# A new table of jobs in the slots of an attention loop, K one batch later, and three pairs of squares on GpSimd

## What is computed

```
x = x + 0.5 * (real(ifft(fft(LN(x)) @ W)) + bias)     # called F1 here
x = x + attention(LN(x))                              # 16 heads of 8, on the left 128 features
x = x + 0.5 * (real(ifft(fft(LN(x)) @ W)) + bias)     # called F2 here
```

## Time and profile before

| | |
|---|---|
| median of three runs | 313.4 us |
| profiled execution | 312.38 us |
| its span | 310.5 us |
| TensorE matmuls busy | 294.8 us (95%) |
| ScalarE busy | 257.6 us (83%) |
| VectorE busy | 190.5 us (61%) |
| GpSimd busy | 98.3 us (32%) |
| granted TensorE clock | full throughout |
| chain that ended last: TensorE / DMA / VectorE / ScalarE | 75% / 9% / 5% / 5% |

### The profile page before, as it was taken

The page is one execution under the profiler, slowest core; times in us unless marked ns, Lnnn a source line. Parts: engine busy times, 40 slices in busy tenths (PEclk is TensorE's granted clock), DMA queues, the critical chain, the costliest instruction groups (busy, mean ns, idle before and its releaser), DMA issues.

```text
span 310.5 us, 8810 instructions
## 1 busy us (share of the span) xinstructions
PE 294.8 (95%) x3440; PEld 112.5 (36%) x3443; DVE 190.5 (61%) x552; ACT 257.6 (83%) x285; POOL 98.3 (32%) x113
## 2 busy tenths in 40 slices
PE   8887999899998999999999999999999999998996
PEld 5633333233332333333333333334333333322333
DVE  1688546747775678657776678567755643370255
ACT  2117998898997889998998989998999999999921
POOL 6562531223604053223604251313600340034005
PEclk9999999999999999999999999999999999999999
DMA  7935615573462762665453663554372464112102
GB/s 192 337 137 192 218 65 153 195 270 133 139 217 83 245 208 103 208 204 217 155 192 129 231 205 112 198 172 143 131 238 104 138 205 170 38 68 70 37 34 70
DMA packets 25891, 49.33 MB, mean 159 GB/s; under 512 B 2032, under 2 KB 14192, under 8 KB 24048
## 3 DMA queue, kind: packets, MB, share of 16 engines
q1 hardware_dynamic: 25152, 48.26, 46.0%
q10 hardware_dynamic: 688, 0.40, 0.8%
HBM read 31.08 MB, written 17.56 MB: 157 GB/s over the span
## 4 chain that ended last, share of the span: by engine, by line
PE 75%; DMA 9%; DVE 5%; ACT 5%; issue 3%; POOL 3%; SPq 0%; ACTq 0%; POOLq 0%
PE ot L828 28%; PE misc L719 26%; PE scores L799 15%; ACT probs L669 5%; DMA leftT<-left_scr 4%; DMA q_scr<-qp 2%; PE scores L719 2%; DMA QS<-q_scr 2%; DMA left_scr<-left_blocks 1%; POOL x L553 1%; PE scores L686 1%; PE scores L693 1%; DVE left_blocks L966 1%; DVE lh L957 1%; POOL rstd L550 1%
## 5 line engine op out<-in xcount | busy, mean ns | idle before, releaser
L669 ACT ACTIVATE probs<-scores 128x1024 f32<-128x1024 f32 x256 | 243.8, 1028 | 20.6 <-PE scores L799 20.3
L828 PE MATMUL ot<-probs,VS 128*32 128x512 f32 x1024 | 133.9, 594 | 2.9 <-ACT probs L669 2.3
L799 PE MATMUL scores<-QS,KS 32*128 32x512 f32 x512 | 64.7, 495 | 3.0 <-DMA QS<-q_scr 1.3
L799 PEld LDWEIGHTS scores<-QS,KS 32*128 32x128 f32 x512 | 24.5, 181 | 109.8 <-ACT probs L669 101.0
L828 PEld LDWEIGHTS ot<-probs,VS 128*32 128x32 f32 x1024 | 30.6, 109 | 25.8 <-ACT probs L669 5.0
L563 POOL TENSOR_TENSOR x_out<-x,half_bias 128x512 f32<-128x512 f32 x7 | 9.0, 1292 | 88.8 <-DVE x L1012 88.8
L548 POOL TENSOR_SCALAR veps<-mv 128x4 f32<-128x4 f32 (+1 forms) x25 | 6.1, 242 | 95.9 <-DVE mv L946 95.9
L1017 DVE SCALAR_TENSOR_TENSOR x_out<-misc,rstd,x_out 128x256 f32<-128x256 f32 x28 | 13.5, 484 | 33.7 <-PE misc L719 30.2
L719 PE MATMUL misc<-half_ffn,xT 128*32 128x256 f32 x448 | 32.1, 386 | 0.0
L719 PE MATMUL misc<-half_ffn,xT_in 128*32 128x256 f32 x400 | 27.1, 385 | 1.4 <-DVE half_ffn L1193 1.3
L550 POOL TENSOR_TENSOR rstd<-veps,power 128x4 f32<-128x4 f32 (+1 forms) x25 | 25.3, 1013 | 2.1
(11 more groups left out here) (125 smaller groups left out, 260.0 us busy)
## 6 DMA issues: line engine op xcount, KB each, us to landing
KS<-k_scr SPq DMA_DIRECT2D x14, 512.0 KB, 4.9
QS<-q_scr SPq DMA_DIRECT2D x14, 512.0 KB, 4.6
x_in<-x SPq DMA_DIRECT2D x8, 512.0 KB, 5.1
xT_in<-x_t SPq DMA_DIRECT2D x8, 512.0 KB, 6.4
k_scr<-kp SPq DMA_DIRECT2D x8, 512.0 KB, 3.0
q_scr<-qp SPq DMA_DIRECT2D x8, 512.0 KB, 4.4
x_scr<-x_blocks SPq DMA_DIRECT2D x7, 512.0 KB, 2.9
xT<-x_scr SPq DMA_DIRECT2D x7, 512.0 KB, 4.7
```

The source lines that it names most:

```text
L669: nc.scalar.activation(probs[u % PRING][:, :, :], scores[u % SRING][:, :, :], ACT.Exp, scale=SCORE_SCALE).then_inc(exp_done, 1)
L799: last = mm(scores[(u + j // 2) % SRING][:, j % 2, :], KS[b % 2][rows, slot, kt * P:(kt + 1) * P].bitcast(F32R), QS[b % 2][rows, slot, :]. ...
L828: last = mm(ot[COL * j:COL * (j + 1), :], VS[b % 2][:, kt, h, :], probs[(u + j // 2) % PRING][:, j % 2, :], start=s % 8 == 0, stop=s % 8 == 7)
```

## The change

The tables are new. Offset 1 is the next batch and 2 the one after it. K of the next batch is made in slots 4 and 6 (STEADY) or 4 and 5 (LATE), where it was made for the batch after the next in slots 14 and 15. F1 and F2 tiles are spread as halves over other slots. SP's loop issues x2 and xT first, then k_out, k_in, q_out and q_in together, and the left half last. The guard's branch moves from slot 12 to 13 in batches 1 to 5, and from 13 to 12 in batch 0. `left_half` goes to slots 12 and 13, the statistics of the next x to slots 6 and 8. The squares of k and q of batches 1, 2 and 7 go from ScalarE to GpSimd; those of batches 3 to 6 stay on ScalarE in slots 8 and 11.

```diff
--- before.py
+++ after.py
@@ -66,28 +66,31 @@
 
 
 
-STEADY = {0: [("F2_3a", -2, LEFT), ("F2_3", -2, LEFT)], 1: [("F1_0a", 2, LEFT), ("F1_0", 2, LEFT)],
+STEADY = {0: [("F2_3", -2, LEFT), ("F1_0a", 2, RIGHT)], 1: [("F1_0", 2, RIGHT)],
           2: [("WO_0", -1, LEFT), ("WO_1", -1, RIGHT)], 3: [("WO_2", -1, LEFT), ("WO_3", -1, RIGHT)],
-          4: [("F1_1a", 2, LEFT), ("F1_1", 2, LEFT)], 5: [("F1_2a", 2, LEFT), ("F1_2", 2, LEFT)],
-          6: [("F1_3a", 2, LEFT), ("F1_3", 2, LEFT)], 7: [("QT_0", 1, LEFT)], 8: [("QT_1", 1, LEFT)],
-          9: [("V_0", 1, RIGHT), ("V_1", 1, LEFT)], 10: [("N", 1, RIGHT), ("F2_0a", -1, LEFT)], 11: [("F2_0", -1, LEFT)],
-          12: [("F2_1a", -1, LEFT), ("F2_1", -1, LEFT)], 13: [("F2_2a", -1, LEFT), ("F2_2", -1, LEFT)],
-          14: [("KT_0", 2, RIGHT)], 15: [("KT_1", 2, RIGHT)]}
-
-FIRST = {**STEADY, 0: [("F1_0a", 2, LEFT), ("F1_0", 2, LEFT)], 1: []}
+          4: [("KT_0", 1, RIGHT), ("F1_1a", 2, LEFT)], 5: [("F1_1", 2, LEFT), ("V_0", 1, RIGHT)],
+          6: [("KT_1", 1, RIGHT), ("F1_2a", 2, LEFT)], 7: [("F1_2", 2, LEFT), ("V_1", 1, RIGHT)], 8: [("QT_0", 1, RIGHT)],
+          9: [("QT_1", 1, RIGHT), ("F1_3a", 2, LEFT)], 10: [("F1_3", 2, LEFT)],
+          11: [("N", 1, RIGHT), ("F2_0a", -1, LEFT)], 12: [("F2_0", -1, LEFT), ("F2_1a", -1, RIGHT)], 13: [("F2_1", -1, RIGHT)],
+          14: [("F2_2a", -1, LEFT), ("F2_2", -1, LEFT)], 15: [("F2_3a", -1, LEFT)]}
+
+FIRST = {**STEADY, 0: [("F1_0a", 2, LEFT), ("F1_0", 2, LEFT)], 1: [("F1_1a", 2, LEFT), ("F1_1", 2, LEFT)],
+         4: [("F1_2a", 2, LEFT)], 5: [("F1_2", 2, LEFT), ("V_0", 1, RIGHT)], 6: [("QT_0", 1, RIGHT)], 7: [("QT_1", 1, RIGHT)],
+         8: [("F1_3a", 2, LEFT)], 9: [("F1_3", 2, LEFT)], 10: [("V_1", 1, RIGHT)]}
 
 BEGIN = {3: [("LT", 1, LEFT)], 4: [("KT_0", 1, RIGHT), ("F1_0a", 2, LEFT)], 5: [("F1_0", 2, LEFT), ("QT_0", 1, RIGHT)],
          6: [("KT_1", 1, RIGHT), ("F1_1a", 2, LEFT)], 7: [("F1_1", 2, LEFT), ("QT_1", 1, RIGHT)],
-         8: [("F1_2a", 2, LEFT), ("F1_2", 2, LEFT)], 9: [("F1_3a", 2, LEFT), ("F1_3", 2, LEFT)],
-         10: [("V_0", 1, RIGHT), ("V_1", 1, LEFT)], 11: [("N", 1, RIGHT)], 12: [("LT", 2, LEFT)],
-         13: [("KT_0", 2, RIGHT)], 14: [("KT_1", 2, LEFT)]}
-
-LATE = {0: [("F2_3a", -2, LEFT), ("F2_3", -2, LEFT)],
+         8: [("F1_2a", 2, LEFT), ("F1_2", 2, LEFT)], 9: [("V_0", 1, RIGHT), ("F1_3a", 2, LEFT)],
+         10: [("F1_3", 2, LEFT), ("N", 1, RIGHT)], 11: [("V_1", 1, RIGHT)],
+         13: [("LT", 2, LEFT)], 14: [("KT_0", 2, RIGHT)], 15: [("KT_1", 2, RIGHT)]}
+
+LATE = {0: [("F2_3", -2, LEFT)],
         2: [("WO_0", -1, LEFT), ("WO_1", -1, RIGHT)], 3: [("WO_2", -1, LEFT), ("WO_3", -1, RIGHT)],
-        5: [("QT_0", 1, LEFT)], 6: [("QT_1", 1, LEFT)], 7: [("V_0", 1, RIGHT)], 8: [("V_1", 1, LEFT)],
-        9: [("F2_0a", -1, LEFT)], 10: [("F2_0", -1, LEFT), ("N", 1, RIGHT)], 11: [("F2_1a", -1, LEFT)], 12: [("F2_1", -1, LEFT)],
-        13: [("F2_2a", -1, LEFT)], 14: [("F2_2", -1, LEFT)]}
-END = {0: [("F2_3a", -2, LEFT), ("F2_3", -2, LEFT)],
+        4: [("KT_0", 1, RIGHT)], 5: [("KT_1", 1, RIGHT)], 6: [("QT_0", 1, RIGHT)], 7: [("QT_1", 1, RIGHT)],
+        8: [("V_0", 1, RIGHT)], 9: [("V_1", 1, RIGHT), ("F2_0a", -1, LEFT)], 10: [("F2_0", -1, LEFT), ("N", 1, RIGHT)],
+        11: [("F2_1a", -1, LEFT)], 12: [("F2_1", -1, LEFT)],
+        13: [("F2_2a", -1, LEFT)], 14: [("F2_2", -1, LEFT)], 15: [("F2_3a", -1, LEFT)]}
+END = {0: [("F2_3", -2, LEFT)],
        2: [("WO_0", -1, LEFT), ("WO_1", -1, RIGHT)], 3: [("WO_2", -1, LEFT), ("WO_3", -1, RIGHT)],
        9: [("F2_0a", -1, LEFT)], 10: [("F2_0", -1, LEFT)], 11: [("F2_1a", -1, LEFT)], 12: [("F2_1", -1, LEFT)],
        13: [("F2_2a", -1, LEFT)], 14: [("F2_2", -1, LEFT)], 15: [("F2_3a", -1, LEFT), ("F2_3", -1, LEFT)]}
@@ -126,7 +129,7 @@
 
 def guard_slot(it):
 
-    return 12 if it else 13
+    return 13 if 0 < it < B - 2 else 12
 
 
 def evac_count(name, b):
@@ -500,31 +503,26 @@
 
             load_x(3)
             k_out(1)
+            q_out(1)
             k_in(1)
-            q_out(1)
             q_in(1)
             for it in range(1, B):
-                if it + 1 < B:
-                    k_out(it + 1)
                 if it >= 2:
                     store_out(it - 2, 1)
                 if it + 3 < B:
                     load_x(it + 3)
-                if it + 1 < B:
-                    k_in(it + 1, slice(0, 1))
                 x2_through(it - 1)
-                if it + 1 < B:
-                    k_in(it + 1, slice(1, None))
                 xT_in_from(it - 1)
                 if it + 1 < B:
+                    k_out(it + 1)
+                    k_in(it + 1)
                     q_out(it + 1)
+                    q_in(it + 1)
                 if it + 2 < B:
                     left_through(it + 2)
-                if it + 1 < B:
-                    q_in(it + 1)
+                store_out(it - 1, 0)
                 if it + 2 < B:
                     leftT_in(it + 2)
-                store_out(it - 1, 0)
             store_out(B - 2, 1)
             store_last_out(B - 1)
             sp.wait_ge(out_stored, 32 * (B - 1) + 16 * T)
@@ -598,13 +596,21 @@
             next_x(2)
             pool.wait_ge(late_loaded, 32)
             begin_x2(0)
+            square(kp, sq_k, kp_step, 1)
+            square(qp, sq_q, qp_step, 1)
             rstd_of(1, 3)
             next_x(3)
             for it in range(1, B):
 
+                if it == 1:
+                    square(kp, sq_k, kp_step, it + 1)
                 end_of(it - 1)
                 rstd_of(2, it)
                 begin_x2(it)
+                if it == B - 2:
+                    square(kp, sq_k, kp_step, it + 1)
+                if it in (1, B - 2):
+                    square(qp, sq_q, qp_step, it + 1)
                 if it + 2 < B:
                     rstd_of(1, it + 3)
                 if it + 3 < B:
@@ -658,11 +664,11 @@
 
             for u in range(PAIRS * B):
                 it, s = divmod(u, PAIRS)
-                if it + 1 < B:
-
-                    if s == (2 * 4 if it else 2 * 8):
+                if 1 < it < B - 2:
+
+                    if s == 2 * 8:
                         square(kp, sq_k, kp_step, it + 1)
-                    if s == (2 * (8 if it == B - 2 else 10) if it else 2 * 9):
+                    if s == 2 * 11:
                         square(qp, sq_q, qp_step, it + 1)
                 act.wait_ge(scores_ready, u // 2 + 1)
                 wait(act, quad_done, (u - PRING) // 2 + 1)
@@ -1248,16 +1254,16 @@
                                 norm_stats(2, x2, t, t == T - 1)
                             norm_moments(2, it)
                     if it + 2 < B:
-                        if s == (8 if it else 10):
+                        if s == 12:
                             left_half(it + 2, range(0, 2))
-                        if s == (9 if it else 10):
+                        if s == (13 if it else 12):
                             left_half(it + 2, range(2, T))
                             if it:
                                 turn_left(it + 2)
                     if it + 3 < B:
-                        if s == 11:
+                        if s == 6:
                             norm0_stats(it + 3, range(0, 2))
-                        if s == 13:
+                        if s == 8:
                             norm0_stats(it + 3, range(2, T))
                             norm_moments(0, it + 4)
                     if s == guard_slot(it) and it + 1 < B:
```

## The result

The changed kernel takes 318.36 us (median of six, 316.31 to 319.91), the kernel before beside it 312.56 us. The ratio is 1.0185, 95% interval 1.0129 to 1.0240: slower by a little under 2%, and the interval takes in the 2% at which a change is called one. The profiled execution is the shortest of the six: 316.3 us, span 314.5, 4.0 more than before.

A forecast was written before the change was run, and what follows sets the result against it. TensorE was taken to set the pace. Slots -3.8, VectorE's two delays +2.7 and Q's round trip +2.7 sum to +1.6 on the profiled 312.4 us: forecast 314.0 us, range 310.0 to 319.0.

The forecast's parts named there:

- the case that I held likeliest: Whole kernel: a small QS wait, 312 to 317 us, chance 0.43, likeliest 314.0.
- The slots: TensorE, all batches: slot prices of the new tables (heavy 2.30, light 1.86) sum to -3.8 us.
- LT where 1.1 was given: Batch 0: LT of batch 2 waits 1.1 us for lh, behind N's chain in VectorE's queue.
- Slot 7's queue: VectorE, slot 7 of batches 2 to 5: ot's transpose is 0.3 us late for slot 8, bounds 0 and 0.6.
- The guard's branch: VectorE, slot 13 of batches 1 to 5: the branch costs 1.2 us, making slot 15 0.3 late, bounds 0 and 0.6.
- The sign that I had named for this step: TensorE: slot 15 at 2.1 us would show VectorE's delay behind the branch.
- QS: SP's queue: Q's round trip through memory makes QS late for slot 15, +2.7 us in all (0 to 10.6).
- rival A: Q comes in time, its store landing within 4.5 us: sum -1.1, 311.3 us; chance 0.33.
- the sign that I had named, a wait for QS once a batch: TensorE at the score products: waits for QS of 0.3 to 1.5 us each from batch 1 on.
- Rival C: Every q store lands at 6.4 us, QS waits are 10.6 in all: 321.9 us; chance 0.15.
- The squares: Squares of k and q moved from ScalarE to GpSimd: cost 0; about 1 us each if their cover were gone.
- rival D: GpSimd's in-order queue holds q's square back and N waits: up to 3 us, 317.0 us; chance 0.04.

The follow-up runs named there:

- r5: Changed kernel with GpSimd's next_x held until lh, and q_out issued before k_in in batches 1 and 6: 311.52 us, ratio 0.997.
- r2: Changed kernel with GpSimd waiting for lh before it makes the next x_in: 316.69 us, ratio 1.012.
- r1: The changed kernel itself, timed and profiled again: 317.98 us, ratio 1.016 against the kernel before.
- r3: Changed kernel with SP issuing q_out before k_in in batches 1 and 6: 313.43 us, ratio 1.003.
- r4: Changed kernel with the squares of batches 1, 2 and 7 back on ScalarE: 317.31 us, ratio 1.013.
- r7: Kernel before with only the squares of batches 1, 2 and 7 moved to GpSimd: 313.41 us, ratio 1.004.
- r9: Changed kernel, next_x after lh, K and Q made earlier in batches 2 to 5, q_out before k_in in all batches: 310.17 us, ratio 0.992.
- r8: r3 with V_1 moved from slot 7 to slot 10 in batches 2 to 5: 317.23 us, ratio 1.011.
- r11: Kernel before with only the statistics of the next x moved from slots 11 and 13 to 6 and 8: 314.04 us, ratio 1.004.
- r6: r5 with V_1 moved to slot 10 in batches 2 to 5, and V_1 and N exchanged in batch 0: 311.76 us, ratio 0.997.

## Why the prediction was right or wrong

The forecast was 314.0, within 310.0 to 319.0; the kernel takes 318.4. The side and the range held, the point was 4.4 too low, and above the 312 to 317 of the case that I held likeliest. Of the 4.4, 1.1 is batch 6 and 2.0 the median over the profile; 1.0 is the start of batch 0, which isn't the change's. The mechanism held in part: two terms stood for something else, and that their sum came out is luck. By its steps:

- **The slots.** The prices held to hundredths: slots 2 to 7, 9 to 13 of batches 2 to 5 are 2.30, 1.86 and 1.95 as added. Batch 1 without its collision takes 33.07 (r5) where 32.98 was summed, batch 7 gained its 0.4, batch 0 waited 0.9 for LT where 1.1 was given. The new STEADY gains next to nothing: that held too.
- **Slot 7's queue.** ot_t was late as worked out: slot 8 takes 2.15 (0.25 for the 0.3 forecast).
- **The guard's branch.** This step failed. I took 1.2 for it from the one row where VectorE waits for "issue". Behind the same branch in slot 13 of batch 2 the issue wait is 0.36, and with the branch left where it is TensorE has no wait in these slots in r2. Batch 5 already says so: it has the branch in slot 13, and its slot 15 takes 1.87. The sign that I had named for this step, slot 15 at 2.1, is there in batches 2 to 4 for another reason. Where the 1.19 of that one row comes from is open.
- **What I left out: GpSimd beside VectorE.** Moving the statistics of the next x to slots 6 and 8 lets GpSimd make the next x_in right behind rstd, in slot 12, where `normalize` and `left_half` now are. The prediction moved VectorE's work and looked at GpSimd only for when it would be done. The price is 0.8 a batch in 2 to 4 and 0.6 in 1, 3.0 in all (r2, r5). By chance that is nearly what I gave to the branch (1.5) and to QS in batches 1 to 5 (1.4) together, which in the first profile of this kernel cost nothing. The +3.0 of batches 2 to 5 and the -1.4 of batch 1 were right for the wrong reason.
- **QS.** The mechanism was right: what is late next is QS, through SP's order. The size was off where it counts. In batches 2 to 5 the store landed in 3.4 to 5.0, about as rival A had it, and each QS was in time; the sign that I had named, a wait for QS once a batch, is not there. Slot 14, longer by 0.5 in batches 2 to 4, gave it some of that time; without that (r5) QS is late in batch 5 alone, by 0.5. In batch 6 the store of Q took 6.1, as taken, but K's store before it 5.6 and not 4.4, and in r1 the loads of QS 5.9 and not 4.9: the wait was 2.1 and 2.9 where 1.3 was given. For K I had taken the median of a row, for a store that was put right behind xT.
- **Beyond the profile.** The runs' median is 2.0 above the profiled execution; the forecast had seen 1.0 for the kernel before and did not use it. r1 shows, in one execution, what that can be: a longer QS wait in batches 1 and 6 and 1.5 of halved clock behind it. r3, which takes away only this wait, is 4.5 faster and scatters less (1.1 for 3.6 and 1.5). Rival C's direction, at another place.
- **The squares** cost nothing on GpSimd in the changed kernel, and gave 0.5 to 0.7 in batch 6 (r4, r7), which the prices of its slots 7 and 8 held. What rival D feared, GpSimd's order, does cost 0.9 when the squares move alone (r7), though it is lh that waits and not N.

## What to carry to other kernels

When a queue's entries are reordered, look at what stands ready behind an entry that must wait: here a store that was ready waited 4 us for another transfer's landing, and exchanging the two was worth 4.5 us of the median, more than the 2.5 us by which the best schedule here (r9) beats the kernel before. When work moves to a time at which another engine is busy on the same memory, price the pair, not each alone: compare one operation's length over all its places in the trace. And ask what stands behind the moved work in the new engine's order. And for a transfer with little margin take its landing from the row with the same neighbours, and count its scatter: a wait that is 2 us in one execution and 3 in the next decides the median.

## What the runs showed of the hardware

Beside a GpSimd addition of 128x512 (1.28 us) some VectorE operations take up to 1 us more: `on`, with two inputs in SBUF, 0.83 and 1.23 (r8) for 0.42, two lh 1.56 for 0.60, one norm_max on 16 numbers 0.89 for 0.18 (r11), a pair of them beside two additions 2.30 for 0.36. Their size doesn't decide: the smallest lost the most. x_out, with one input in PSUM, keeps its 0.48, and the reciprocal, with one input, its 0.34. GpSimd's rstd of 128x4 held up neither norm_max (0.36 the pair) nor lh (0.59 the pair in r11).

A TensorE wait of 2.9 us (r1) was followed by some 3 us at a granted clock of 0.50, which cost 1.5 us more. The length of the wait alone doesn't decide: 2.1 us in the first profile and 3.6 us in r2 were not followed by it, 2.2 us in r8 and 1.3 us in r6 were (there the slot of LT took 4.44). What does is open.

A store of 512 KB landed 2.9 us (K, batch 5) to 6.3 us (Q, batch 1) after its issue in the changed kernel, 5.6 right behind xT and 6.1 to 6.3 right behind K's two loads.
